# The second weight matrix scaled and centred along its rows, ahead of its transpose, in a two-layer hypergraph block

## The chip, the cores and the metric

The kernel runs on one core of a Trainium2 chip. Its five engines each work through their own instructions in order and meet only at semaphores: TensorE (PE in the profile), VectorE (DVE), ScalarE (ACT), GpSimd (POOL) and SyncE (SP, which here only issues transfers). The metric is the device time of one execution in microseconds (us), as the median of three runs.

## What is computed

The reference, cut to what matters. There are 64 graphs of 128 nodes, with 256 features in and out and 512 hidden ones. All is float32.

```python
def hypergraph_conv(x, adj, W, b):
    H = (adj != 0).astype(x.dtype)
    w = adj.reshape(N, -1)[:, :C]             # the first row of adj
    xw = jnp.einsum('ncd,hd->nch', x, W)
    Dn = 1 / einsum('nce,ne->nc', H, w)       # 0 where the sum is not positive
    Be = 1 / H.sum(axis=1)                    # 0 where the sum is 0
    m = Be[:, :, None] * jnp.einsum('nce,nch->neh', H, xw)
    return Dn[:, :, None] * jnp.einsum('nce,neh->nch', H, m) + b

h = relu(hypergraph_conv(x, adj, W1, b1))
h = (h - mean(h)) * rsqrt(var(h) + EPS_LN) * gamma + beta
y = hypergraph_conv(h, adj, W2, b2) + x
out = _layernorm(x + y)
```

The part that the change touches works on the weights alone. Since the normalised h is multiplied by W2, gamma can be folded into W2 (W2 times gamma, column by column), the subtraction of the mean of h can be folded in too (each output row of the scaled W2 less its own mean over the 512 hidden units), and beta gives one constant vector of 256 values, c2 = W2 beta, that is added to every row.

## The kernel before

The 64 graphs go in 16 groups of 4 (G, PER). For each group the kernel makes H, its transpose ht_sb, the matrix A = D H B H^T (make_s, then make_a, then transposed into at_sb), u = x^T A (make_u), v = W1 u (make_v, four chunks k of 128 hidden units, each six passes in a split of every operand into a high and a low half), r = relu(v) (ACT, L564), its split into r_hi (POOL, L1025) and r_lo (DVE, L751), g = r W2 (make_g, one call for each of the 4 graphs, 12 passes each, eight with r_hi and four with r_lo), the statistics of r from squares (sq_sb, pair_sb, q_sb, turn_q), y = A g (make_y), and the normalised output. Every engine's program is one list written out by hand; nothing reorders it. Groups are staggered: make_v of the next group is put between the make_g of this one.

Ahead of the loop stands a ramp, which fills this pipeline and prepares the weights. W1 is transposed (turn_w1) and split. W2 arrives as w2_raw with its 256 output rows in two blocks c of 128 partitions. In the kernel before, PE transposes it (turn_w2, L360) into PSUM; DVE multiplies by gamma on the way to w2_g (scale_w2, L806), since after the transpose the hidden unit is the partition and gamma a column of vec; the mean over the hidden units is then a sum over partitions, for which DVE adds the four chunks into one (w2_sum, L888 and L891), PE multiplies by a matrix of ones (sum_w2, L397) and DVE subtracts (centre_w2, L813); ACT rounds to w2_hi (L636) and DVE takes the rest, w2_lo (L819, w2_ready). c2 is made by PE from w2_t, the unscaled transpose that ACT copies out of PSUM (L631), and from beta_b, beta spread along the free axis by POOL (L1057): four matrix products (make_c2, L404), read by DVE (L824). b1, gamma and beta come by three small transfers, one transpose and one copy (vec).

In the PE program the ramp ends with make_v(0, 2), sum_w2, make_v(0, 3), make_c2 for two chunks, make_s(1), make_c2 for two chunks; then it waits for w2_ready, and the first make_g follows. Within the first pass of the loop (i = 0) stand turn_a(1), turn_h(2) and make_u(1) between the make_g, then turn_q(0), make_v(1, 0) and make_s(2).

Two waits stand at the join of ramp and loop. make_g of graph 0 waits chunk by chunk for r_hi and, in its last four passes, for r_lo of chunks 0 to 3. And relu(0, 3) on ACT must be done before POOL can make the fourth r_hi, after which DVE makes the fourth r_lo.

Of the kernel before, what the change touches and what calls it, by code (L numbers as in the profile page):

```python
# [5 lines left out]
ALU = mybir.AluOpType  # L6
# [5 lines left out]
P = 128  # L12
# [8 lines left out]
def hypergraph_block(nc, x, adj, W1, b1, gamma, beta, W2, b2, out):  # L21
# [13 lines left out]
    with ExitStack() as ctx:  # L35
# [15 lines left out]
        vec_rows = sb("vec_rows", [3 * KH, P])  # L51
        vec = sb("vec", [P, 3 * KH])
        w1_hi = sb("w1_hi", [P, KD, HID], F32R)
        w1_lo = sb("w1_lo", [P, KD, HID], F32R)
        w2_t = sb("w2_t", [P, KH, DOUT])
        w2_g = sb("w2_g", [P, KH, DOUT])
        w2_sum = sb("w2_sum", [P, KH // 2, DOUT])
        beta_b = sb("beta_b", [P, KH, P])
# [58 lines left out]
        turned_q = bank_g[:, PER - 1]  # L117

# [54 lines left out]
        def _(sp):  # L173
# [43 lines left out]
            load_x(1)  # L217
            sp.dma_start(b2_half[:, :], b2.unsqueeze(0).to_broadcast([P, DOUT])).then_inc(weights_in[3], 16)
# [30 lines left out]
        def _(pe):  # L249
# [41 lines left out]
            def make_v(i, k):  # L291
                if i == 0 and k < 2:
                    pe.wait_ge(w1_ready, k + 1)
                    pe.wait_ge(u_hi_ready, 1)
                elif k < 2:
# [87 lines left out]
            def make_first_u():  # L383
                pe.wait_ge(first_at, 1)
                pe.wait_ge(x_in[0], 16)
                for c in range(KD):
                    pe.wait_ge(vec_ready if c else edges_ready, 1)
                    for n in range(PER):
                        if n == PER // 2:
                            pe.wait_ge(at_ready, 1)  # L390
                        mm = pe.matmul(bank_g[:, c, graph(n)], x_sb[:, 0, n, graph(c)], at_sb[:, 0, n],  # L391
                                       start=True, stop=True)
                    mm.then_inc(u_made, 1)

            def sum_w2():
                pe.wait_ge(w2_added, 2)
                pe.matmul(bank_g[:, 0, 0:DOUT], ones[:, :], w2_sum[:, 0], start=True,  # L397
                          stop=True).then_inc(w2_summed, 1)
# [714 lines left out]
```

## Time and profile before

| | us |
|---|---|
| median of 3 runs | 284.51 (284.22 to 284.69) |
| the profiled execution, its own time | 284.18 |
| its span, first to last instruction | 282.4 |
| PE busy | 274.3 |
| DVE busy | 228.8 |
| ACT busy | 197.5 |
| POOL busy | 135.0 |

The span is the stretch in which the profile shows instructions; the execution's own time is 1.8 us longer. Busy time is the union of an engine's instructions. A timeline row gives the start, the duration, the engine, the line and the operation, the destination tile and the sources, and in brackets how long the engine had been idle before and what ended that. Names in it drop a tile's numbers: w_hi is w1_hi or w2_hi, c is c2, w_bn is w2_bn. A row that says x2 merges neighbours, and each float32 product shows as more than one pass. An instruction's recorded duration contains its latency, so the next one on the same engine can start some 0.05 to 0.1 us before its end.

### The profile page before, as it was taken

How to read it: one execution, taken by the hardware profiler on the slowest of the kernel's cores; microseconds unless marked ns; L12 is line 12 of the kernel's file. 1: busy time of each engine (PE TensorE's matmuls, PEld its weight loads, DVE VectorE, ACT ScalarE, POOL GpSimd, SP SyncE). 2: the span in 40 equal slices, each digit the busy share in tenths (PEclk: the TensorE clock that was granted, in tenths of full speed). 3: DMA queues.
4: the chain of work that ended last, by engine and by line, in shares of the span. 5: the costliest groups of instructions: out<-in, count | busy, mean ns of one | idle time of the engine just before them, and what ended most of it. 6: DMA issues, size and time to landing. Idle time of an engine off the chain costs nothing.

```text
span 282.4 us, 5790 instructions
## 1 busy us (share of the span) xinstructions
PE 274.3 (97%) x1820; PEld 249.1 (88%) x1820; DVE 228.8 (81%) x646; ACT 197.5 (70%) x561; POOL 135.0 (48%) x196
## 2 busy tenths in 40 slices
PE   7999999999999999999999999999999999999991
PEld 6889899898999989898998989899898989889891
DVE  3795689797878979797987979797897969797784
ACT  3588967877777787776767877677778776564733
POOL 2332546436363744536274553536364363627372
PEclk9999999999999999999999999999999999999997
DMA  6922041334324334433433533523323242120024
GB/s 216 329 56 76 3 130 37 95 113 131 115 59 138 84 93 120 127 114 84 144 62 99 134 100 112 124 85 56 126 63 93 79 111 77 37 74 3 1 75 149
DMA packets 37302, 27.70 MB, mean 98 GB/s; under 512 B 10060, under 2 KB 35352, under 8 KB 37272
## 3 DMA queue, kind: packets, MB, share of 16 engines
q1 hardware_dynamic: 37024, 27.17, 33.9%
q8 instruction: 14, 0.23, 0.4%
q10 hardware_dynamic: 248, 0.17, 0.2%
q14 instruction: 16, 0.13, 0.2%
HBM read 17.21 MB, written 8.42 MB: 91 GB/s over the span
## 4 chain that ended last, share of the span: by engine, by line
PE 86%; DVE 5%; ACT 4%; POOL 2%; issue 2%; POOLq 0%; DVEq 0%; ACTq 0%
PE bank_v L309 29%; PE bank_g L326 10%; PE bank_g L319 9%; PE bank_g L321 9%; PE bank_v L287 9%; PE bank_v L345 9%; PE bank_s L267 4%; PE bank_g L338 2%; PE bank_s L410 1%; DVE r_lo L751 1%; ACT ht_sb L513 1%; ACT sq_sb L571 1%; DVE pair_sb L756 1%; ACT r_sb L564 1%; PE bank_g L391 1%
## 5 line engine op out<-in xcount | busy, mean ns | idle before, releaser
L1017 POOL TENSOR_TENSOR xb_sb<-x_sb,b_half 128x512 f32<-128x512 f32 (+1 forms) x31 | 41.1, 1327 | 70.7 <-DVE r_lo L751 53.7
L564 ACT ACTIVATE r_sb<-bank_v,vec 128x512 f32<-128x512 f32 x64 | 44.2, 691 | 38.5 <-PE bank_v L309 37.9
L319 PE MATMUL bank_g<-w_hi,r_hi 128*128 128x258 f32 x256 | 66.8, 293 | 0.0
L1025 POOL TENSOR_SCALAR r_hi<-r_sb 128x512 fp32r<-128x512 f32 x64 | 43.8, 684 | 42.6 <-ACT r_sb L564 42.1
L321 PE MATMUL bank_g<-w_lo,r_hi 128*128 128x256 f32 x256 | 63.7, 281 | 0.0
L309 PE MATMUL bank_v<-u_lo,w_hi 128*128 128x512 f32 x128 | 50.8, 397 | 0.0
L309 PE MATMUL bank_v<-u_hi,w_lo 128*128 128x512 f32 x128 | 50.8, 397 | 0.0
L309 PE MATMUL bank_v<-u_hi,w_hi 128*128 128x512 f32 x128 | 50.7, 396 | 0.0
L319 PEld LDWEIGHTS bank_g<-w_hi,r_hi 128*128 128x128 f32 x256 | 48.3, 189 | 1.7 <-DVE w_lo L819 0.3
L321 PEld LDWEIGHTS bank_g<-w_lo,r_hi 128*128 128x128 f32 x256 | 48.2, 188 | 1.2
L751 DVE TENSOR_TENSOR r_lo<-r_sb,r_hi 128x512 fp32r<-128x512 f32 x64 | 48.7, 782 | 0.5 <-POOL r_hi L1025 0.5
L326 PE MATMUL bank_g<-w_hi,r_lo 128*128 128x258 f32 x256 | 42.1, 285 | 0.1
L571 ACT ACTIVATE sq_sb<-r_sb 128x512 f32<-128x512 f32 x64 | 40.2, 635 | 1.9
L742 DVE SCALAR_TENSOR_TENSOR g_sb<-bank_g,rstd,c 128x256 f32<-128x256 f32 x62 | 27.2, 480 | 12.2 <-POOL rstd L1001 12.2
L326 PEld LDWEIGHTS bank_g<-w_hi,r_lo 128*128 128x128 f32 x256 | 35.8, 189 | 0.5 <-DVE r_lo L751 0.5
L576 ACT ACTIVATE z_sb<-z_sb,shift,rstd 128x256 f32<-128x256 f32 x60 | 32.3, 587 | 2.7 <-POOL shift L1039 2.7
L542 ACT ACTIVATE u_hi<-bank_v 128x512 fp32r<-128x512 f32 x30 | 17.9, 601 | 21.6 <-PE bank_v L287 21.6
L1001 POOL TENSOR_TENSOR rstd<-stat,half_power 128x2 f32<-128x2 f32 x31 | 21.9, 708 | 17.3 <-DVE stat L732 17.2
L287 PE MATMUL bank_v<-at_sb,x_sb 128*128 128x128 f32 x240 | 29.5, 276 | 0.0
L309 PEld LDWEIGHTS bank_v<-u_lo,w_hi 128*128 128x128 f32 x128 | 24.0, 188 | 6.1 <-DVE u_lo L719 0.7
L345 PE MATMUL bank_v<-g_sb,at_sb 128*128 128x256 f32 x120 | 28.8, 380 | 0.0
L287 PEld LDWEIGHTS bank_v<-at_sb,x_sb 128*128 128x128 f32 x240 | 28.0, 192 | 0.5 <-issue 0.5
(124 smaller groups left out, 453.6 us busy)
## 6 DMA issues: line engine op xcount, KB each, us to landing
x_sb<-in_x_dram SPq DMA_DIRECT2D x16, 512.0 KB, 3.9
out_dram<-z_sb SPq DMA_DIRECT2D x14, 512.0 KB, 3.3
adj_sb<-in_adj_dram SPq DMA_DIRECT2D x15, 256.0 KB, 4.2
d_row<-d_rows SPq DMA_DIRECT2D x13, 256.0 KB, 3.7
w_raw<-in_L_gnn_W_dram SPq DMA_DIRECT2D x2, 512.0 KB, 4.9
out_dram<-z_sb SPq DMA_DIRECT2D x3, 256.0 KB, 2.1
adj_sb<-in_adj_dram SPq DMA_DIRECT2D x2, 128.0 KB, 2.3
turned_h<-h_sb SPq DMA_TRANSPOSE x13, 2.4
```

Of the source, the lines that this page charges most:

```text
L287: mm = pe.matmul(bank_v[:, c, graph(n)], x_sb[:, j % 3, n, graph(c)], at_sb[:, j % 3, n], start=True, stop=True)
L309: mm = pe.matmul(bank_v[:, k % 2], w[:, c, graph(k)], u[:, c], start=(m == 0), stop=(m == len(terms) - 1))
L319: pe.matmul(bank_g[:, n, 0:W2COLS], r_hi[:, i % 2, k, graph(n)], w2_hi[:, k], start=(k == 0), stop=False)
L321: pe.matmul(bank_g[:, n, 0:DOUT], r_hi[:, i % 2, k, graph(n)], w2_lo[:, k], start=False, stop=False, skip_group_check=True)
L326: mm = pe.matmul(bank_g[:, n, 0:W2COLS], r_lo[:, i % 2, k, graph(n)], w2_hi[:, k], start=False, stop=(k == KH - 1))
L345: mm = pe.matmul(bank_v[:, half, (n % 2) * DOUT:(n % 2 + 1) * DOUT], at_sb[:, i % 3, n], g_sb[:, n], start=True, stop=True)
L564: nc.scalar.activation(r_sb[:, k], bank_v[:, k % 2], ACT.Relu, bias=vec[:, k:k + 1]).then_inc(relu_ready, 1)
L571: nc.scalar.activation(sq_sb[:, k], r_sb[:, k], ACT.Square).then_inc(sq_ready, 1)
L576: ins = nc.scalar.activation(z_sb[:, i % 2, n], z_sb[:, i % 2, n], ACT.Identity, bias=shift2[:, n:n + 1], scale=rstd2[:, 0, n:n + 1])
L751: nc.vector.tensor_tensor(r_lo[:, i % 2, k], r_sb[:, k], r_hi[:, i % 2, k].bitcast(F32), ALU.subtract).then_inc(r_lo_ready, 1)
L1017: nc.gpsimd.tensor_tensor(xb_sb[:, i % 2, part], x_sb[:, i % 3, part], b2_half[:, :].unsqueeze(1).to_broadcast([P, n, DOUT]), ALU.add).the ...
L1025: nc.gpsimd.tensor_scalar(r_hi[:, i % 2, k], r_sb[:, k], 1.0, 1.0, ALU.mult, ALU.mult).then_inc(r_hi_ready, 1)
```

## The change

- **Loads.** gamma and beta are each loaded onto all 128 partitions (gamma_b, beta_b, 128x512) by SP, and only b1 comes by the small transfer. W2 comes in two transfers, one for each block of output rows. The order on SP is now: the two halves of adj 0, W1, gamma_b, x 0, adj 1, W2 block 0, W2 block 1, adj 2, x 1, beta_b, b2, and on as before.
- **W2.** POOL multiplies w2_raw by gamma_b (two TENSOR_TENSOR of 128x512). DVE takes each row's mean (mean_w2: one bn_stats over 512 and one bn_aggr for each block). POOL subtracts it (two TENSOR_SCALAR). PE transposes the finished matrix once (turn_w2), ACT rounds it out of PSUM to w2_hi, DVE takes w2_lo out of PSUM.
- **c2.** POOL multiplies w2_raw by beta_b. DVE takes row means (bn_stats, bn_aggr) and writes for each block a diagonal matrix with 512 times the mean (c2_diag). PE multiplies ones by the two diagonals (make_c2), which puts c2 on all partitions.
- **Orders.** make_first_u does both chunks of the first two graphs, then both of the last two. make_first_v replaces make_v(0, 0) and make_v(0, 1) and interleaves them. turn_h(1) stands ahead of them. turn_w2 moves behind make_v(0, 2), make_s(1) ahead of make_v(0, 3), turn_h(2) and turn_a(1) ahead of the first make_g, make_u(1) ahead of the second. make_c2 stands behind turn_q(0). The lists of ACT, DVE and POOL follow.

The core of the diff (the new tiles, semaphores and make_first_u are left out):

```diff
-            sp.dma_start(w2_raw[:, :, :], W2.rearrange("(k p) h -> p k h", p=P)).then_inc(weights_in[2], 16)
+            sp.dma_start(gamma_b[:, :], gamma.unsqueeze(0).to_broadcast([P, HID])).then_inc(gamma_in, 16)
             load_x(0)
             load_adj(1)
+            for c in range(KD):
+                sp.dma_start(w2_raw[:, c], W2[c * P:(c + 1) * P, :]).then_inc(w2_high_in if c else weights_in[2], 16)
...
-            def turn_w2(half):
-                pe.wait_ge(weights_in[2], 16)
+            def turn_w2(c):
+                pe.wait_ge(w2_centred, c + 1)
                 pe.wait_ge(ht_ready, 1)
...
+                for k in range(KH):
+                    mm = pe.transpose(w2_turned_in[:, k, graph(c)], w2_g[:, c, graph(k)], ident[:, :])
...
+            def make_c2():
+                pe.wait_ge(diag_ready, KD)
+                pe.wait_ge(at_ready, 2)
                 for c in range(KD):
...
+                    mm = pe.matmul(bank_q[:, graph(c)], ones[:, :], c2_diag[:, c], start=True, stop=True)
+                mm.then_inc(c2_made, 1)
...
             turn_first_a(0)
+            turn_first_a(1)
+            make_first_u()
+            turn_h(1)
+            make_first_v()
+            make_v(0, 2)
             turn_w2(0)
-            turn_first_a(1)
             turn_w2(1)
-            make_first_u()
-            make_v(0, 0)
-            turn_h(1)
-            make_v(0, 1)
-            make_v(0, 2)
-            sum_w2()
+            make_s(1)
             make_v(0, 3)
-            make_c2([0, 1])
-            make_s(1)
-            make_c2([2, 3])
+            turn_h(2)
+            turn_a(1)
...
             relu(0, 0)
-            read_ht(1)
             relu(0, 1)
...
+            make_htb(1)
             relu(0, 2)
-            make_htb(1)
-            act.wait_ge(w2_centred, 1)
-            nc.scalar.activation(w2_hi[:, :, 0:DOUT], w2_g[:, :, :], ACT.Copy).then_inc(w2_hi_ready, 1)
+            act.wait_ge(w2_turned, KD)
+            nc.scalar.activation(w2_hi[:, :, 0:DOUT], w2_turned_in, ACT.Copy).then_inc(w2_hi_ready, 1)
+            make_a(1)
             relu(0, 3)
-            make_a(1)
             read_at(1)
...
+            def sum_beta(c):
+
+                dve.wait_ge(beta_scaled, c + 1)
+                nc.vector.bn_stats(w2_bn[:, 1, c], w2_beta[:, c]).then_inc(c2_step, 1)
...
+            pool.wait_ge(gamma_in, 16)
+            for c in range(KD):
+                pool.wait_ge(w2_high_in if c else weights_in[2], 16)
+                nc.gpsimd.tensor_tensor(w2_g[:, c], w2_raw[:, c], gamma_b[:, :], ALU.mult).then_inc(w2_scaled, 1)
+            for c in range(KD):
+                pool.wait_ge(w2_mean_ready, c + 1)
+                nc.gpsimd.tensor_scalar(w2_g[:, c], w2_g[:, c], w2_mv[:, 0, c, 0:1], 1.0, ALU.subtract,
+                                        ALU.mult).then_inc(w2_centred, 1)
             for k in range(KH):
...
+                split_r(0, k)
+            pool.wait_ge(beta_in, 16)
+            for c in range(KD):
+                nc.gpsimd.tensor_tensor(w2_beta[:, c], w2_raw[:, c], beta_b[:, :], ALU.mult).then_inc(beta_scaled, 1)
```

PE before, from the last pass of make_v(0, 3) to the first make_g (w_t is w2_t, L404 is make_c2, L267 make_s(1)):

```order
L309 MATMUL bank_v<-u_lo,w_hi 128x512
L404 MATMUL bank_g<-w_t,beta_b 128x256 [waits w2_t_ready,beta_ready]
L404 MATMUL bank_g<-w_t,beta_b 128x256
L267 MATMUL bank_s<-htb_sb,ht_sb 128x129 [waits a_ready,at_ready,wcol_ready,htb_ready]
L267 MATMUL bank_s<-htb_sb,ht_sb 128x129 x3
L404 MATMUL bank_g<-w_t,beta_b 128x256 [waits w2_t_ready,beta_ready]
L404 MATMUL bank_g<-w_t,beta_b 128x256
L319 MATMUL bank_g<-w_hi,r_hi 128x258 [waits r_hi_ready,w2_ready]
```

PE now, from the last pass of make_v(0, 2) to the first of make_v(0, 3): the products for c2 are gone from here, W2's one transpose and make_s(1) stand ahead of make_v(0, 3).

```order
L311 MATMUL bank_v<-u_lo,w_hi 128x512
L361 MATMUL bank_g<-ident,w_g 128x128 [waits ht_ready,w2_centred]
L361 MATMUL bank_g<-ident,w_g 128x128 x3
L361 MATMUL bank_g<-ident,w_g 128x128 [waits ht_ready,w2_centred]
L361 MATMUL bank_g<-ident,w_g 128x128 x3
L276 MATMUL bank_s<-htb_sb,ht_sb 128x129 [waits a_ready,at_ready,wcol_ready,htb_ready]
L276 MATMUL bank_s<-htb_sb,ht_sb 128x129 x3
L311 MATMUL bank_v<-u_hi,w_hi 128x512 [waits relu_ready]
```

The products for c2, four of 128x256, are two of 128x128 now and stand behind turn_q(0).

POOL before, from beta_b to the first xb_sb:

```order
L1057 TENSOR_SCALAR beta_b<-ones,vec 128x128 [waits vec_ready,consts_ready]
L1057 TENSOR_SCALAR beta_b<-ones,vec 128x128 x3
L1061 TENSOR_SCALAR b_half<-b_half 128x256 [waits weights_in3]
L1063 TENSOR_SCALAR ident<-ident 128x128
L1025 TENSOR_SCALAR r_hi<-r_sb 128x512 [waits relu_ready,consts_ready]
L1025 TENSOR_SCALAR r_hi<-r_sb 128x512 [waits relu_ready] x3
L995 COPY htb_sb<-edge_cols 128x4 [waits s_made,edges_ready] x2
L1017 TENSOR_TENSOR xb_sb<-x_sb,b_half 128x512 [waits q_ready,x_in0]
L1017 TENSOR_TENSOR xb_sb<-x_sb,b_half 128x512 [waits b_ready]
```

POOL now, from the scaling of W2 to the first two xb_sb (w_g is w2_g, w_beta is w2_beta):

```order
L1064 TENSOR_TENSOR w_g<-w_raw,gamma_b 128x512 [waits weights_in2,gamma_in]
L1064 TENSOR_TENSOR w_g<-w_raw,gamma_b 128x512 [waits w2_high_in]
L1067 TENSOR_SCALAR w_g<-w_g,w_mv 128x512 [waits w2_mean_ready] x2
L1032 TENSOR_SCALAR r_hi<-r_sb 128x512 [waits relu_ready] x4
L1073 TENSOR_TENSOR w_beta<-w_raw,beta_b 128x512 [waits beta_in]
L1073 TENSOR_TENSOR w_beta<-w_raw,beta_b 128x512
L1075 TENSOR_SCALAR b_half<-b_half 128x256 [waits weights_in3]
L1077 TENSOR_SCALAR ident<-ident 128x128
L1002 COPY htb_sb<-edge_cols 128x4 [waits s_made,edges_ready,consts_ready]
L1002 COPY htb_sb<-edge_cols 128x4 [waits s_made,edges_ready]
```

The two products with gamma and the two subtractions stand ahead of the four r_hi of group 0, and the two products with beta right behind them.

DVE before, from the third and fourth r_lo of group 0 to the sum of squares:

```order
L751 TENSOR_TENSOR r_lo<-r_sb,r_hi 128x512 [waits r_hi_ready] x2
L824 COPY c<-bank_g 128x256 [waits c2_made]
L692 TENSOR_SCALAR h_sb<-adj_sb 128x512 [waits h_turned,adj_in0]
L711 TENSOR_SCALAR binv<-members 128x4 [waits ht_ready]
L714 RECIPROCAL binv<-binv 128x4 [waits htb_ready,b_step]
L756 TENSOR_TENSOR pair_sb<-sq_sb 128x512 [waits sq_ready] x2
L763 TENSOR_TENSOR q_sb<-pair_sb 128x512 [waits pairs_ready]
```

DVE now, from the fourth r_lo to the same place:

```order
L760 TENSOR_TENSOR r_lo<-r_sb,r_hi 128x512 [waits r_hi_ready]
L825 BN_STATS w_bn<-w_beta 128x6 [waits beta_scaled]
L827 BN_AGGR w_mv<-w_bn 128x2 [waits c2_step]
L829 TENSOR_SCALAR c_diag<-ident,w_mv 128x128 [waits c2_mean_ready]
L825 BN_STATS w_bn<-w_beta 128x6 [waits beta_scaled]
L827 BN_AGGR w_mv<-w_bn 128x2 [waits c2_step]
L829 TENSOR_SCALAR c_diag<-ident,w_mv 128x128 [waits c2_mean_ready]
L720 TENSOR_SCALAR binv<-members 128x4 [waits ht_ready]
L723 RECIPROCAL binv<-binv 128x4 [waits htb_ready,b_step]
L765 TENSOR_TENSOR pair_sb<-sq_sb 128x512 [waits sq_ready] x2
```

Six instructions for c2 stand between the fourth r_lo and the binv of group 2, ahead of the pairs of squares.

## Rows read from the trace of the kernel before

**Rows 1.** The profile page, first part: busy time, share of the span, instructions.

```profile
PE 274.3 (97%) x1820; PEld 249.1 (88%) x1820; DVE 228.8 (81%) x646; ACT 197.5 (70%) x561; POOL 135.0 (48%) x196
```

**Rows 2.** Busy time by stretch: window, length, then each engine's busy time and instructions.

```profile
60.00:100.00 40.00, 39.97 (x269) 36.72 (x268) 33.86 (x102) 29.16 (x88) 21.50 (x29) 1.00 0.35 98
```

**Rows 3.** Timeline of PE in the ramp: start us, us, line, operation, out<-in, count.

```profile
9.74 1.95 PE L391 MATMUL bank_g<-at_sb,x_sb 128*128 128x128 f32 x16
...
16.54 0.59 PE L397 MATMUL bank_g<-w_sum,ones 128*128 128x256 f32 x2
...
18.36 1.02 PE L404 MATMUL bank_g<-w_t,beta_b 128*128 128x256 f32 x4
19.22 1.06 PE L267 MATMUL bank_s<-htb_sb,ht_sb 128*128 128x129 f32 x8
20.11 1.03 PE L404 MATMUL bank_g<-w_t,beta_b 128*128 128x256 f32 x4
21.06 0.39 PE L319 MATMUL bank_g<-w_hi,r_hi 128*128 128x258 f32 x1
...
22.96 0.60 PE L275 MATMUL bank_s<-ident,a_sb 128*128 128x128 f32 x4
...
23.60 0.36 PE L319 MATMUL bank_g<-w_hi,r_hi 128*128 128x258 f32 x1
...
25.11 1.95 PE L287 MATMUL bank_v<-at_sb,x_sb 128*128 128x128 f32 x16
26.82 0.37 PE L319 MATMUL bank_g<-w_hi,r_hi 128*128 128x258 f32 x1
...
28.81 0.66 PE L338 MATMUL bank_g<-ident,q_sb 128*128 128x128 f32 x4 [0.32 <-DVE q_sb L763]
29.41 0.50 PE L309 MATMUL bank_v<-u_hi,w_hi 128*128 128x512 f32 x1
...
30.91 1.05 PE L267 MATMUL bank_s<-htb_sb,ht_sb 128*128 128x129 f32 x8
```

**Rows 4.** The chain that ended last, one piece: start us, us, what.

```profile
33.41 4.19 PE bank_v L309 x18
```

**Rows 5.** Timeline of ACT in the ramp, columns as in the third group.

```profile
10.84 0.60 ACT L542 ACTIVATE u_hi<-bank_g 128x512 fp32r<-128x512 f32 x1 [0.38 <-PE bank_g L391]
...
13.70 0.69 ACT L564 ACTIVATE r_sb<-bank_v,vec 128x512 f32<-128x512 f32 x1 [1.38 <-PE bank_v L309]
...
18.69 1.06 ACT L636 ACTIVATE w_hi<-w_g 128x1024 fp32r<-128x1024 f32 x1
...
21.52 1.14 ACT L530 ACTIVATE a_sb<-bank_s,dinv 128x128 f32<-128x128 f32 x4 [1.20 <-DVE dinv L706]
```

**Rows 6.** Timeline of DVE in the ramp and after it.

```profile
10.04 0.43 DVE L692 TENSOR_SCALAR h_sb<-adj_sb 128x512 bf16<-128x512 f32 x1 [0.47 <-DMA adj_sb<-in_adj_dram]
...
16.23 1.10 DVE L751 TENSOR_TENSOR r_lo<-r_sb,r_hi 128x512 fp32r<-128x512 f32 x1
...
21.40 1.28 DVE L751 TENSOR_TENSOR r_lo<-r_sb,r_hi 128x512 fp32r<-128x512 f32 x2
...
38.65 1.10 DVE L756 TENSOR_TENSOR pair_sb<-sq_sb 128x512 f32<-128x512 f32 x1
...
45.36 1.38 DVE L785 BATCH_NORM_STATS2 bn_sb<-z_sb 128x6 f32<-128x256 f32 x4
```

**Rows 7.** Timeline of POOL at the same places.

```profile
16.10 0.69 POOL L1025 TENSOR_SCALAR r_hi<-r_sb 128x512 fp32r<-128x512 f32 x1 [0.94 <-ACT r_sb L564]
...
21.43 1.30 POOL L995 COPY htb_sb<-edge_cols 128x4 f32<-128x4 f32 x2
...
38.40 0.81 POOL L1025 TENSOR_SCALAR r_hi<-r_sb 128x512 fp32r<-128x512 f32 x1 [0.65 <-ACT r_sb L564]
39.16 0.64 POOL L995 COPY htb_sb<-edge_cols 128x4 f32<-128x4 f32 x1
```

**Rows 8.** Groups of POOL's instructions with their shapes: count, busy us, mean ns.

```profile
L1017 POOL TENSOR_TENSOR xb_sb<-x_sb,b_half 128x512 f32<-128x512 f32 x30 | 38.7, 1292 | 68.0 <-DVE r_lo L751 53.7 <-DVE binv L714 8.1 <-DVE q_sb L763 6.2
```

More of the change, by code:

```diff
@@ L50, in hypergraph_block @@
         w2_raw = sb("w2_raw", [P, KD, HID])
-        vec_rows = sb("vec_rows", [3 * KH, P])
-        vec = sb("vec", [P, 3 * KH])
+        vec_rows = sb("vec_rows", [KH, P])
+        vec = sb("vec", [P, KH])
         w1_hi = sb("w1_hi", [P, KD, HID], F32R)
         w1_lo = sb("w1_lo", [P, KD, HID], F32R)
[L55 to L58, printed above, removed]
+        gamma_b = sb("gamma_b", [P, HID])
+        beta_b = sb("beta_b", [P, HID])
+        w2_g = sb("w2_g", [P, KD, HID])
+        w2_beta = sb("w2_beta", [P, KD, HID])
+        w2_bn = sb("w2_bn", [P, 2, KD, 6])
+        w2_mv = sb("w2_mv", [P, 2, KD, 2])
+        c2_diag = sb("c2_diag", [P, KD, P])
         w2_hi = sb("w2_hi", [P, KH, W2COLS], F32R)
@@ L291, in make_v @@
             def make_v(i, k):
[L292 to L295, printed above, removed]
+                if k < 2:
                     pe.wait_ge(u_lo_ready, i * KD + (k + 1))
@@ L385, in make_first_u @@
                 pe.wait_ge(x_in[0], 16)
-                for c in range(KD):
[L387 to L398, printed above, removed]
@@ L400, in make_c2 @@
-            def make_c2(chunks):
-                pe.wait_ge(beta_ready, 1)
-                pe.wait_ge(w2_t_ready, 1)
-                for k in chunks:
-                    mm = pe.matmul(bank_g[:, 1, 0:DOUT], beta_b[:, k], w2_t[:, k], start=(k == 0), stop=(k == KH - 1))
-                if chunks[-1] == KH - 1:
-                    mm.then_inc(c2_made, 1)
+                for half in range(2):
+                    for c in range(KD):
+                        if half:
+                            pe.wait_ge(at_ready, 1)
+                        else:
+                            pe.wait_ge(vec_ready if c else edges_ready, 1)
+                        for n in each(half):
+                            mm = pe.matmul(bank_g[:, c, graph(n)], x_sb[:, 0, n, graph(c)], at_sb[:, 0, n],
+                                           start=True, stop=True)
+                        if half:
+                            mm.then_inc(u_made, 1)
@@ new lines, in make_first_v, with add @@
+            def make_first_v():
+                def add(k, c, w, u, first=False, last=False):
+                    return pe.matmul(bank_v[:, k], w[:, c, graph(k)], u[:, c], start=first, stop=last,
+                                     skip_group_check=True)
+                pe.wait_ge(u_hi_ready, 1)
+                for k in range(2):
+                    pe.wait_ge(w1_ready, k + 1)
+                    add(k, 0, w1_hi, u_hi, first=True)
+                    add(k, 0, w1_lo, u_hi)
+                pe.wait_ge(u_lo_ready, 1)
+                for k in range(2):
+                    add(k, 0, w1_hi, u_lo)
+                pe.wait_ge(u_hi_ready, KD)
+                for k in range(2):
+                    add(k, 1, w1_hi, u_hi)
+                    add(k, 1, w1_lo, u_hi)
+                    pe.wait_ge(u_lo_ready, KD)
+                    add(k, 1, w1_hi, u_lo, last=True).then_inc(v_made, 1)
@@ L443, in _ @@
                 if i == 0:
-                    turn_a(1)
-                    turn_h(2)
-                    pe.wait_ge(c2_ready, 1)
+                    make_u(1)
                 make_g(i, 1)
-                if i == 0:
-                    make_u(1)
                 if i == LAST:
@@ L605, in _ @@
             act.dma_start(edge_rows[:, :], adj[:, 0, :]).then_inc(edges_in, 16)
[L606 to L608 removed]
+            act.dma_start(vec_rows[:, :], b1.rearrange("(k p) -> k p", p=P)).then_inc(weights_in[0], 16)
             act.wait_ge(consts_ready, 2)
@@ L1064, in _ @@
             pool.wait_ge(consts_ready, 5)
-            for k in range(KH):
-                split_r(0, k)
             copy_w(2)
```

92 lines of the change are left out of this document (37 added, 55 removed).

## The prediction, made before the changed kernel ran

> **What bounds the kernel now.** I read the share of busy time first: PE is busy for 274.3 of 282.4 us [rows 1]. Then the stretches: in the loop it is busy 39.97 of 40 us [rows 2], so there PE's own list is the time, and the change leaves the loop behind its first pass alone. What it can move is the ramp. So I read PE's timeline there and set a checkpoint that both kernels pass with the same PE work done and the same work left: the start of make_s(2), at 30.91 us [rows 3]. Whatever the changed kernel is earlier or later there, I carry unchanged to the end; a full PE list neither gives it back nor adds to it.
>
> **What the change takes from PE.** sum_w2 starts at 16.54 and make_v(0, 3) follows at 16.78, about 0.24 us; the next pass runs only after a wait for a relu, so another 0.2 there. The products for c2 hold 18.36 to 19.22 and 20.11 to 21.06, 0.86 + 0.95 = 1.81 us [rows 3]. The two new products of 128x128 are four passes like those of turn_a, which takes 22.96 to 23.40, 0.44 us [rows 3]. So PE has 0.24 + 1.81 - 0.44 = 1.6 us less to do. The eight transposes of W2 only move. The rest of the working is on how much of the 1.6 comes back as waiting.
>
> **The start.** SP now issues gamma_b (256 KB) where it issued W2 (512 KB), so x 0 and adj 1 come no later; adj 1 was used on landing at 10.04 [rows 6]. W2's blocks follow behind it, 256 KB each; from 10.0 on I give each about 0.9 us. On POOL a two-input product of 128x512 takes 1.29 us [rows 8]: blocks scaled by 11.5 and 12.8 or, with 0.5 us of lateness, 13.3. DVE comes to the first mean only behind u_lo, at about 13.0, so loads and scaling are covered by up to 1.4 us and cost nothing. On PE turn_w2 is gone ahead of make_first_u, which starts at 9.5 instead of 9.74 [rows 3], but its first chunk is complete only after 12 of 16 passes, not 8: u_hi starts at 11.05 instead of 10.84 [rows 5]. The twelve passes of make_first_v run from 11.8 at 0.233 us each (18 in 4.19 us, [rows 4]), without the old waits in between. relu(0, 0) starts at 14.25 where it started at 13.70, takes 0.69 [rows 5], and make_v(0, 2) waits for it: 15.1 to 16.5.
>
> **The middle, a chain through four engines.** DVE's mean: a bn_stats of 128x256 is a quarter of 1.38 us [rows 6], so 0.67 for 512 elements, and 0.2 for the small bn_aggr. The two means are done at 13.8 and 14.9, POOL's subtractions at 14.5 and 15.6 to 15.8 (0.62 us each, as an r_hi [rows 7]). PE wants the second at 16.9, so this is covered too. Then turn_w2 16.5 to 17.4, make_s(1) 0.89 us to 18.25, make_v(0, 3) to 19.65. The sums of make_s(1) are out at 18.5, three small DVE operations end at 19.1, make_a(1) takes 1.14 us [rows 5]. Because it now stands ahead of relu(0, 3) on ACT, that relu runs 20.1 to 20.8, although its input was ready at 19.95. turn_h(2) waits for the same make_a(1), 0.7 us of idle PE; turn_a(1) is done at 21.1. w2_hi and w2_lo come at 18.6 and 20.2 (their operations took 1.06 and 1.23 us) and are ahead of that. POOL makes the fourth r_hi by 21.5; make_h(3) is on DVE at the time, which may hold it up to 21.75.
>
> **The step that decides.** Right behind the fourth r_hi POOL starts the product with beta_b; DVE is to make the fourth r_lo, from two inputs in SBUF. In the trace POOL and DVE don't run such pairs side by side. The r_lo at 16.23 takes 1.10 us instead of 0.68, beside an r_hi from 16.10 to 16.79 [rows 6, 7]: it ends 0.54 after the other. The pair_sb at 38.65 does the same after the r_hi that ends at 39.21. Whoever comes second waits for the first's end. POOL starts its next instruction just ahead of its last one's end (0.05 us: 38.40 + 0.81 against 39.16 [rows 7]) while DVE must be told first. So POOL gets in, with an operation of 1.29 us: 21.7 to 23.0, and the fourth r_lo ends at 23.3 to 23.55. The trace has no such DVE instruction beside a POOL TENSOR_TENSOR of this size. The bounds for this wait are 0 (it runs undisturbed, ending at 22.5) and both POOL products, 2.55 us. I take one product, 1.25, since the pair_sb at 38.65 got its turn at the end of one instruction, ahead of the copy that POOL had begun at 39.16, which ended only at 39.80, after it [rows 6, 7].
>
> The Trainium skill, page "SBUF — State Buffer", section "Who interferes with whom", says that a DVE instruction with two SBUF inputs and a GpSimd instruction that reads SBUF exclude each other for the whole instruction, and that the one that issues first wins. The rows above agree at 0.62 us, and the page makes no exception for products; by it the wait is the 1.25 us that I take, without it the sum below would be 0.7 us better. It does not say who is next of two that wait.
>
> **From there to the checkpoint.** With the fourth r_lo at 23.5 the first make_g ends at 23.7. Before, it was followed by turn_a and turn_h and all were done at 23.60 [rows 3]: so the gain is used up, 0.1 us behind. make_u(1) takes 1.71 and a make_g 1.51 (25.11 to 26.82, 23.60 to 25.11): make_u and two make_g end at 23.7 + 4.73 = 28.45. Before, PE reached turn_q(0) only at 28.81, after 0.32 us of waiting for q_sb, and make_v(1, 0) at 29.41 behind u_lo [rows 3]. Now: c2's second product ends at 24.8 on POOL, DVE's six operations (2 x (0.67 + 0.2 + 0.25)) at 26.15, binv at 26.45, pairs and sum (3 x 0.6) at 28.3. So q_sb is just in time and turn_q(0) runs 28.45 to 28.9. The c2 products follow to 29.35, by when the first u_lo (28.9) is there. make_v(1, 0) takes 6 x 0.233 = 1.4 to 30.75, where it took 1.50. That is 0.16 us ahead of 30.91. Reading c2 on DVE ends at 29.9 and is covered by make_v(1, 0). At the profiled execution this gives 284.18 - 0.16 = 284.02; the median of the runs lies 0.33 above that execution, so I forecast 284.35.
>
> **The rivals.**
> - **No exclusion by a product.** The fourth r_lo ends at 22.5, one us earlier. Then the sum of squares becomes the bound: c2's DVE operations end at 25.45, q_sb at 27.65, turn_q(0) and c2 until 28.65, make_v(1, 0) until 30.05: 0.86 ahead, 283.65. Against it are rows of the same pair at a smaller size; for it, that the trace has no such case.
> - **POOL keeps its turn through both products (the other side).** In DVE's own case it is so: two r_lo run 21.40 to 22.68 back to back while POOL's copies wait from 21.43 to 22.73 [rows 6, 7]. If POOL does the same, the fourth r_lo ends at 24.8, the first make_g at 25.0, and the two make_g behind make_u(1) at 29.75, turn_q(0) and c2 at 30.65, make_v(1, 0) at 32.05: 1.14 behind, 285.65. It decides as soon as the second product starts ahead of the r_lo. Against it stands the copy at 39.16.
> - **The weights come late.** If the scaled block 0 isn't there at 13.0, every us beyond that moves the means, and beyond some 1.1 us for block 1 the transposes; the r_hi stand behind them on POOL. At 2 us of lateness this costs about 0.9, 285.4.
> - **The change doesn't do what it says**, in that PE's freed 1.6 us are waited away earlier and the exclusion adds to it, because the chain make_s(1), make_a(1), relu(0, 3) is longer than counted. Each 0.1 us there is 0.1 us at the end; this is the width of the main case, not a case of its own.
>
> **How the numbers follow.** Chances: the main case 0.60, no exclusion 0.22, POOL keeps its turn 0.13, late weights 0.05. In the main case some ten hand-overs are added up, the holding up by make_h(3) is 0 or 0.25, and adding a few tenths each way gives 283.8 to 284.9. The predicted time is the likeliest case's, 284.35. The range reaches into both others, 283.3 to 285.3: it leaves out most of the slower cases and the better half of an even larger gain, about 0.2. A measurement of this kernel tells 0.2%, 0.57 us, from no change. Faster by more than that: 0.12 of the main case and most of the second, 0.19, together 0.31. Slower by more: 0.05 of the main case and most of the last two, 0.15, together 0.20. Within it: 0.49.
>
> **What would show it.** The profile of the changed kernel should have the fourth r_lo of group 0 at 1.7 to 1.9 us instead of 0.68, beginning just behind POOL's first product with beta_b and ending about 0.54 after it. With 0.68 there the first rival holds, with 3 us the second. PE should stand idle some 0.7 us ahead of turn_h(2) and about one us within the first make_g, and make_s(2) should start at 30.7 or 30.8. turn_w2 without a wait shows that loads and means are covered. turn_q(0) should wait less than 0.2 us. A make_s(2) that is as forecast and a time that isn't would prove the carrying to the end wrong; a relu(0, 3) that begins before 19.9 or after 20.5 would prove the middle wrong.

## The result: 1.5 us slower, outside the range

The changed kernel takes 286.07 us (median of 4 runs, 285.95 to 286.24), the kernel before beside it 284.60 (4 runs, 284.22 to 284.71). The ratio is 1.0058, with a 95% interval of 1.0046 to 1.0070. (The ratios here and below are not the quotients of the two medians beside them and differ from those by up to 0.13%.) The forecast was 284.35 with a range of 283.3 to 285.3; the profiled execution of after took 285.95 us, with a span of 284.1. The busy shares, in the page's first part:

```profile
PE 272.1 (96%) x1814; PEld 247.8 (87%) x1814; DVE 230.0 (81%) x646; ACT 197.0 (69%) x560; POOL 142.0 (50%) x198
```

PE is busy 2.2 us less than in [rows 1], so what was to go (1.6 us by the forecast) is gone, and the span is 1.7 us longer. POOL is busy 7.0 us more, with 198 instructions instead of 196. The ramp on PE (start us, us, line, operation, tiles, count, and in brackets the idle time ahead and who ended it):

```profile
16.50 0.60 PE L361 MATMUL bank_g<-ident,w_g 128*128 128x128 f32 x4
18.06 0.66 PE L361 MATMUL bank_g<-ident,w_g 128*128 128x128 f32 x4 [0.96 <-POOL w_g L1067]
18.55 1.06 PE L276 MATMUL bank_s<-htb_sb,ht_sb 128*128 128x129 f32 x8
...
22.54 0.38 PE L266 MATMUL bank_s<-ident_b,h_sb 128*128 128x128 bf16 x4 [1.54 <-ACT a_sb L544]
...
25.62 0.39 PE L328 MATMUL bank_g<-w_hi,r_lo 128*128 128x258 f32 x1 [0.95 <-DVE r_lo L760]
25.84 1.95 PE L296 MATMUL bank_v<-at_sb,x_sb 128*128 128x128 f32 x16
...
30.52 0.60 PE L340 MATMUL bank_g<-ident,q_sb 128*128 128x128 f32 x4
30.95 0.61 PE L423 MATMUL bank_s<-c_diag,ones 128*128 128x128 f32 x4
...
32.79 1.05 PE L276 MATMUL bank_s<-htb_sb,ht_sb 128*128 128x129 f32 x8
```

The checkpoint, the last row, stands at 32.79 against 30.91 in [rows 3]: 1.88 us later. Between turn_w2 and the checkpoint PE waits three times: 0.96 between the two halves of turn_w2, 1.54 ahead of turn_h(2), 0.95 ahead of the last pass of the first make_g. POOL at the same place, which [rows 7] shows of before:

```profile
11.21 2.54 POOL L1064 TENSOR_TENSOR w_g<-w_raw,gamma_b 128x512 f32<-128x512 f32 x2 [5.54 <-DMA w_raw<-in_L_gnn_W_dram]
14.01 3.99 POOL L1067 TENSOR_SCALAR w_g<-w_g,w_mv 128x512 f32<-128x512 f32 x2 [0.26 <-DVE w_mv L815]
17.97 2.22 POOL L1032 TENSOR_SCALAR r_hi<-r_sb 128x512 fp32r<-128x512 f32 x3
23.05 0.71 POOL L1032 TENSOR_SCALAR r_hi<-r_sb 128x512 fp32r<-128x512 f32 x1 [2.86 <-ACT r_sb L578]
23.73 2.97 POOL L1073 TENSOR_TENSOR w_beta<-w_raw,beta_b 128x512 f32<-128x512 f32 x2
```

The second row is the surprise: two subtractions of the mean hold POOL for 3.99 us, 2.0 us each. The prediction had 0.62 each. The second ends at 18.00, and the three r_hi, two of which had their input from ACT by 15.6 and the third by 17.4, stand behind it. DVE (compare [rows 6]):

```profile
13.01 0.68 DVE L813 BATCH_NORM_STATS2 w_bn<-w_g 128x6 f32<-128x512 f32 x1
13.73 0.18 DVE L815 BATCH_NORM_AGGREGATE w_mv<-w_bn 128x2 f32<-128x6 f32 x1
...
14.89 0.41 DVE L701 TENSOR_SCALAR h_sb<-adj_sb 128x512 bf16<-128x512 f32 x1
18.63 2.11 DVE L760 TENSOR_TENSOR r_lo<-r_sb,r_hi 128x512 fp32r<-128x512 f32 x2 [3.33 <-POOL r_hi L1032]
...
21.05 0.16 DVE L715 SCALAR_TENSOR_TENSOR dinv<-bank_s,degree 128x4 f32<-128x4 f32 x1
...
23.79 1.77 DVE L760 TENSOR_TENSOR r_lo<-r_sb,r_hi 128x512 fp32r<-128x512 f32 x1 [0.51 <-POOL r_hi L1032]
```

DVE stands idle for 3.33 us until the first r_hi is there. Then two r_lo, held up by r_hi beside them, take 2.11 us and stand ahead of degree and dinv. So make_a(1) on ACT starts at 21.25 and relu(0, 3) behind it at 22.27 (compare [rows 5]):

```profile
14.26 1.32 ACT L578 ACTIVATE r_sb<-bank_v,vec 128x512 f32<-128x512 f32 x2 [0.97 <-PE bank_v L401]
...
21.25 1.14 ACT L544 ACTIVATE a_sb<-bank_s,dinv 128x128 f32<-128x128 f32 x4 [1.47 <-DVE dinv L715]
22.27 0.71 ACT L578 ACTIVATE r_sb<-bank_v,vec 128x512 f32<-128x512 f32 x1
```

Around and behind the checkpoint the delay stays what it is: turn_q of the 16 groups starts 1.71 us later than before for the first and 1.6 to 1.82 later for the others. The two profiled executions differ by 1.77 us (285.95 against 284.18), 0.11 less than the checkpoint; the two medians differ by 1.47, since the profiled execution of before is 0.42 below its median and that of the changed kernel only 0.12.

### The profile page after: what moved, and what is told of

It reads as the page before. It is cut to its first block, busy times and chain, and to the rows that moved or that the text cites. A ratio compares the mean times of both kernels' runs of the same rounds, so it can differ in the third digit from the quotient of the medians.

```text
span 284.1 us, 5774 instructions
## 1 busy us (share of the span) xinstructions
PE 272.1 (96%) x1814; PEld 247.8 (87%) x1814; DVE 230.0 (81%) x646; ACT 197.0 (69%) x560; POOL 142.0 (50%) x198
## 4 chain that ended last, share of the span: by engine, by line
PE 84%; DVE 5%; POOL 4%; issue 2%; DMA 2%; ACT 1%; SPq 1%; POOLq 0%; DVEq 0%
PE bank_v L311 28%; PE bank_g L328 10%; PE bank_g L321 10%; PE bank_g L323 10%; PE bank_v L296 9%; PE bank_v L347 9%; PE bank_s L276 4%; PE bank_g L340 2%; DMA x_sb<-in_x_dram 2%; POOL w_g L1067 1%; DVE r_lo L760 1%; POOL r_hi L1032 1%; POOL rstd L1039 1%; PE bank_g L393 1%; DVE bn_sb L976 1%
## 5 line engine op out<-in xcount | busy, mean ns | idle before, releaser
L760 DVE TENSOR_TENSOR r_lo<-r_sb,r_hi 128x512 fp32r<-128x512 f32 x64 | 50.4, 808 | 4.3 <-POOL r_hi L1032 4.3
L311 PE MATMUL bank_v<-u_hi,w_hi 128*128 128x512 f32 x124 | 49.3, 398 | 0.1
L311 PE MATMUL bank_v<-u_lo,w_hi 128*128 128x512 f32 x124 | 49.1, 396 | 0.0
L311 PE MATMUL bank_v<-u_hi,w_lo 128*128 128x512 f32 x124 | 49.0, 395 | 0.0
L311 PEld LDWEIGHTS bank_v<-u_lo,w_hi 128*128 128x128 f32 x124 | 23.3, 188 | 5.3
```

What stands on the lines that cost most here:

```text
L311: mm = pe.matmul(bank_v[:, k % 2], w[:, c, graph(k)], u[:, c], start=(m == 0), stop=(m == len(terms) - 1))
L760: nc.vector.tensor_tensor(r_lo[:, i % 2, k], r_sb[:, k], r_hi[:, i % 2, k].bitcast(F32), ALU.subtract).then_inc(r_lo_ready, 1)
```

## The experiments

**What POOL's subtraction costs.** The changed kernel with eleven operations put behind the last of POOL's program, each waiting for the one ahead of it, with DVE and ACT done; its total time says nothing.

```diff
+            form(dst, src, 1.0, 1.0, ALU.mult, ALU.mult)
+            form(dst, src, point, 1.0, ALU.mult, ALU.mult)
+            form(dst, src, point, 1.0, ALU.subtract, ALU.mult)
+            form(dst, src, 1.0, 1.0, ALU.subtract, ALU.mult)
+            form(dst, src, 1.0, 1.0, ALU.add, ALU.mult)
+            form(dst, src, point, 1.0, ALU.add, ALU.mult)
...
+            form(dst, src, point, None, ALU.subtract, None)
```

> The changed kernel with eleven more GpSimd TENSOR_SCALAR instructions behind its last one, one after another, on tiles that nothing uses any more; only their durations count, not the time. In the changed kernel the two subtractions (pointer scalar, subtract then mult, in place, 128x512) took 3.99 us together, an r_hi (immediates, mult then mult) 0.62. If the pointer scalar is the price: the mult with a pointer takes 1.3 to 2.0, a subtract or an add with an immediate 0.62. If the operation is the price: subtract with an immediate takes 2.0, mult with a pointer at most 1.3 (four of 128x128 took 1.60 in the kernel before). If working in place is the price: the same subtraction out of place takes 0.6 to 0.7.

Its timeline of POOL, each row one operation of 128x512, in the order of the diff (the scalar is the number 1.0 or, where mv_sb is among the inputs, one value for each partition):

```profile
281.73 0.62 POOL L1113 TENSOR_SCALAR sq_sb<-sq_sb 128x512 f32<-128x512 f32 x1 [0.75 <-DVE z_sb L994]
282.45 0.69 POOL L1113 TENSOR_SCALAR sq_sb<-sq_sb,mv_sb 128x512 f32<-128x512 f32 x1
283.24 2.00 POOL L1113 TENSOR_SCALAR sq_sb<-sq_sb,mv_sb 128x512 f32<-128x512 f32 x1
285.33 1.92 POOL L1113 TENSOR_SCALAR sq_sb<-sq_sb 128x512 f32<-128x512 f32 x1
287.34 0.62 POOL L1113 TENSOR_SCALAR sq_sb<-sq_sb 128x512 f32<-128x512 f32 x1
288.05 0.69 POOL L1113 TENSOR_SCALAR sq_sb<-sq_sb,mv_sb 128x512 f32<-128x512 f32 x1
...
292.94 1.57 POOL L1111 TENSOR_SCALAR sq_sb<-sq_sb,mv_sb 128x512 f32<-128x512 f32 x1
```

The value read from a partition costs 0.07 us, addition nothing, subtraction 1.3 us, whether it takes the number or the value. In place it takes 2.00 as well; at 128x128 it takes 0.72 where a product takes 0.37; as the instruction's only operation, with no product behind it, 1.57. So the price belongs to the operation subtract on this engine, not to the value per partition and not to working in place. Each form ran once; the two subtractions of the kernel itself, taken singly, show 2.01 and 2.00.

**The subtractions on DVE.** This and the next two kernels ran beside the kernel before at 284.24 us (19 runs).

```diff
                 nc.vector.bn_aggr(w2_mv[:, 0, c], w2_bn[:, 0, c]).then_inc(w2_mean_ready, 1)
+                dve.wait_ge(w2_mean_ready, c + 1)
+                nc.vector.tensor_scalar(w2_g[:, c], w2_g[:, c], w2_mv[:, 0, c, 0:1], None,
+                                        ALU.subtract).then_inc(w2_centred, 1)
...
-            for c in range(KD):
-                pool.wait_ge(w2_mean_ready, c + 1)
-                nc.gpsimd.tensor_scalar(w2_g[:, c], w2_g[:, c], w2_mv[:, 0, c, 0:1], 1.0, ALU.subtract,
-                                        ALU.mult).then_inc(w2_centred, 1)
```

> The changed kernel with the two subtractions of the mean on VectorE, right behind each mean, instead of on GpSimd. Theory that the mis-sized subtraction is the whole miss: the transpose of block 1 starts at 16.9 without a wait (18.06 in the changed kernel), the first r_hi at 15.0 (17.97), relu(0, 3) at 20.1 (22.27), make_s(2) at 30.8 (32.79), and the time is 286.07 - 2.0 = 284.1. Rival, that the exclusion beside the products with beta and the order of ACT hold the rest: only the 0.96 us of PE idle ahead of the transpose go, time 285.1.

284.45 us (10 runs, 284.00 to 284.82), ratio 0.9994 (0.9980 to 1.0009), against the 284.1 expected: the slowdown is gone, and so is any gain. DVE's row and PE's rows:

```profile
14.51 0.49 DVE L817 TENSOR_SCALAR w_g<-w_g,w_mv 128x512 f32<-128x512 f32 x1
...
22.17 1.77 DVE L760 TENSOR_TENSOR r_lo<-r_sb,r_hi 128x512 fp32r<-128x512 f32 x1 [0.51 <-POOL r_hi L1035]
```

```profile
10.13 2.02 PE L393 MATMUL bank_g<-at_sb,x_sb 128*128 128x128 f32 x16 [0.66 <-issue]
...
17.05 1.03 PE L361 MATMUL bank_g<-ident,w_g 128*128 128x128 f32 x8
```

The eight transposes stand in one row without a wait, and the fourth r_lo still takes 1.77. But make_first_u begins at 10.13, where the forecast had 9.5: x 0 was late. That is the next thing to explain (below).

**POOL's products with beta behind the fourth r_lo**, in the changed kernel and in the last one.

```diff
             pool.wait_ge(beta_in, 16)
+            pool.wait_ge(r_lo_ready, KH)
             for c in range(KD):
```

> The changed kernel with one more wait: GpSimd's products with beta start only when all four r_lo of group 0 are done. The fourth r_lo takes 0.68 instead of 1.77. Theory: the gain of 1.1 us there is lost at the sum of squares, since the products end 0.4 later and DVE's six operations for c2 stand ahead of it; PE waits about 1.1 us at turn_q(0), which starts at 30.5 to 30.7 (30.52), time 286.0. Rival, that the first make_g alone decides: make_s(2) 1.0 earlier, 285.1.

> Both edits together: the subtractions on VectorE, and the products with beta behind the four r_lo. Theory: as the first edit alone, 284.1, since the sum of squares is what comes last in both; turn_q(0) at 28.4 to 28.6. Rival, that the exclusion costs its 1.1 us at the end: 283.1.

They took 286.48 (4 runs, ratio 1.0075, 1.0060 to 1.0090) and 284.66 (10 runs, 1.0018, 1.0006 to 1.0031), where 286.0 and 284.1 were expected, and neither is better than its base. In the first:

```profile
24.14 0.69 DVE L760 TENSOR_TENSOR r_lo<-r_sb,r_hi 128x512 fp32r<-128x512 f32 x1 [0.51 <-POOL r_hi L1032]
```

```profile
31.03 0.66 PE L340 MATMUL bank_g<-ident,q_sb 128*128 128x128 f32 x4 [1.09 <-DVE q_sb L772]
```

With nothing of POOL beside it the r_lo takes 0.69, so the 1.77 was the product's doing. But the us is handed on, as expected: the products, the sums for c2 and q_sb come later, and PE waits 1.09 for q_sb, as it waits 1.08 in the second of the two. (The start of turn_q(0), 31.03, isn't to be held against the 30.52 of the changed kernel as it stands: this profiled execution begins make_first_u at 9.90, 0.34 later.)

**POOL adds the negated mean.** This and the next two ran beside the kernel before at 284.33 us (25 runs). DVE makes -mean (128x1, 0.15 us) and POOL keeps the work.

```diff
-                nc.gpsimd.tensor_scalar(w2_g[:, c], w2_g[:, c], w2_mv[:, 0, c, 0:1], 1.0, ALU.subtract,
+                nc.gpsimd.tensor_scalar(w2_g[:, c], w2_g[:, c], w2_neg[:, c:c + 1], 1.0, ALU.add,
```

> The changed kernel with the subtraction left on GpSimd, but done as the addition of the negated mean (one more small VectorE operation for each block). With the operation as the price, the two take 0.69 us each instead of 2.0, and the time is that of the kernel with the subtractions on VectorE, 284.3 to 284.7. With the pointer or the working in place as the price they stay at 2.0 and the time at 286.1.

284.55 us (10 runs, 284.22 to 285.00), ratio 1.0005 (0.9995 to 1.0014), as expected. An addition in place of the subtraction takes back the 1.5 us. This is the cleanest pair here, since both profiled executions begin make_first_u at nearly the same time (9.63 and 9.56) and POOL's list has the same order in both: the checkpoint stands at 31.14 against 32.79, 1.65 us earlier.

```profile
14.27 0.70 POOL L1071 TENSOR_SCALAR w_g<-w_g,w_neg 128x512 f32<-128x512 f32 x1 [0.47 <-DVE w_neg L818]
15.54 0.82 POOL L1071 TENSOR_SCALAR w_g<-w_g,w_neg 128x512 f32<-128x512 f32 x1 [0.56 <-DVE w_neg L818]
```

**gamma behind x 0 and adj 1**, with the subtractions on DVE. The issues of the first x_sb, with size and time to landing in us, in this order: the kernel before, the changed kernel, the one with the subtractions on DVE, and this one:

```profile
x_sb<-in_x_dram SPq DMA_DIRECT2D x1, 512.0 KB, 6.3
```

```profile
x_sb<-in_x_dram SPq DMA_DIRECT2D x1, 512.0 KB, 6.7
```

```profile
x_sb<-in_x_dram SPq DMA_DIRECT2D x1, 512.0 KB, 7.2
```

```profile
x_sb<-in_x_dram SPq DMA_DIRECT2D x1, 512.0 KB, 5.6
```

The same window of before and of the kernel with the subtractions on DVE (window, length, PE busy, granted clock, DMA share, GB/s):

```profile
6.00:8.00 2.00, 1.88 (x17) 1.00 1.01 339
```

```profile
6.00:8.00 2.00, 1.93 (x18) 1.00 0.90 224
```

gamma_b is among the loads under way in this window. It is half the size of W2's, which stood there before, but each of 128 partitions fetches the same row of HBM, and the core's whole traffic falls from 339 to 224 GB/s (247 in the changed kernel). With gamma's load later the slow window moves with it, from 6 to 8 (298 GB/s there) to 8 to 10:

```profile
8.00:10.00 2.00, 1.67 (x12) 1.00 0.92 246
```

The kernels with gamma ahead of x 0 have 322 to 363 GB/s from 8 to 10. And the landing isn't chance: in all six profiled executions with gamma ahead x 0 lands 6.7 to 7.2 us after its issue, in all three with gamma behind 5.4 to 5.6. Of before there is one profile, with 6.3 behind twice the bytes; against it this load holds up x 0 by 0.4 to 0.9 us.

```diff
-            sp.dma_start(gamma_b[:, :], gamma.unsqueeze(0).to_broadcast([P, HID])).then_inc(gamma_in, 16)
             load_x(0)
             load_adj(1)
+            sp.dma_start(gamma_b[:, :], gamma.unsqueeze(0).to_broadcast([P, HID])).then_inc(gamma_in, 16)
```

> The kernel with the subtractions on VectorE, and gamma's load onto all partitions issued behind x 0 and adj 1 instead of ahead of them. There x 0 landed 7.2 us after its issue, at 10.0, where it landed at 9.1 in the kernel before, and make_first_u started at 10.13. Theory that the broadcast holds the queue longer than its 256 KB tell: x 0 lands by 8.8, make_first_u starts at 9.5, bound by at_sb, and everything behind is 0.6 earlier: 283.9. Rival, that x 0's landing is chance from run to run: no difference, 284.45.

284.13 us (10 runs, 283.88 to 284.48), ratio 0.9995 (0.9986 to 1.0005). That is between the 283.9 of the theory and the 284.45 of its rival, and the time alone doesn't decide; the landing and the checkpoint, at 30.51 and 0.65 earlier than with gamma first, do. Of before the checkpoint is 0.40 ahead, which the runs can't tell from nothing.

```profile
30.51 1.05 PE L276 MATMUL bank_s<-htb_sb,ht_sb 128*128 128x129 f32 x8
```

**The products with beta in gaps of POOL.** To the last kernel: the first product ahead of the first r_hi, the second between the third and the fourth, and beta loaded ahead of x 1.

```diff
             pool.wait_ge(beta_in, 16)
             for k in range(KH):
+                if k in (0, KH - 1):
+                    c = k // (KH - 1)
+                    nc.gpsimd.tensor_tensor(w2_beta[:, c], w2_raw[:, c], beta_b[:, :],
+                                            ALU.mult).then_inc(beta_scaled, 1)
                 split_r(0, k)
```

> The kernel with gamma's load later, and the two products with beta moved into gaps of GpSimd: the first ahead of the first r_hi, the second between the third and the fourth r_hi; beta's load is issued one place earlier. Theory: the fourth r_lo takes 0.68 instead of 1.77 and the operations for c2 are no later than before, so PE neither waits 0.95 in the first make_g nor at turn_q(0), and make_s(2) is 1.0 to 1.1 earlier than in the kernel with gamma's load later: 282.9 if that one is at 283.9. Rival, that the products in the gaps hold up the first r_hi or the third r_lo by as much: no difference.

283.80 us (10 runs, 283.05 to 284.25), ratio 0.9976 (0.9965 to 0.9987): faster than the kernel before, by a quarter of a per cent, the best of all here, but 0.9 us above the 282.9 expected. make_s(2) starts at 30.33, only 0.18 earlier than in the kernel with gamma's load later, where 1.0 to 1.1 was expected: what the fourth r_lo no longer loses is lost elsewhere, as the rival had it. Its timelines of DVE and PE:

```profile
14.45 1.25 DVE L720 TENSOR_SCALAR binv<-members 128x4 f32<-128x4 f32 x1
...
22.23 0.88 DVE L760 TENSOR_TENSOR r_lo<-r_sb,r_hi 128x512 fp32r<-128x512 f32 x1 [0.51 <-POOL r_hi L1035]
```

```profile
17.28 0.66 PE L361 MATMUL bank_g<-ident,w_g 128*128 128x128 f32 x4 [0.30 <-DVE w_g L817]
```

The fourth r_lo takes 0.88, and the last pass of the first make_g doesn't wait. But binv, an operation on four numbers a partition, takes 1.25 us instead of 0.16 because it met the first product (14.20 to 15.66), and the second mean stands behind it.

**The first product moved behind the second r_hi**, to spare binv (beside the kernel before at 284.60, 17 runs).

```diff
-                if k in (0, KH - 1):
-                    c = k // (KH - 1)
+                if k in (KH - 2, KH - 1):
+                    c = k - (KH - 2)
```

> The kernel before this one (beta_in_gaps, 283.8) with POOL's first product with beta moved from ahead of the first r_hi to behind the second, where POOL stood idle 0.97 us in the kernel with gamma issued later; the second product stays ahead of the fourth r_hi. Nothing else is changed. My theory: what that kernel lost was binv (L720), which took 1.25 us instead of 0.16 because it met the first product, and with it the second mean, the transposes and make_a(1), 0.5 to 0.7 us in all; the fourth r_lo was no longer held up. So here binv is 0.16 us again, the eight transposes stand without a wait, the fourth r_lo takes 0.69 to 0.9 us and ends at 22.3 to 22.6 instead of 23.1, make_s(2) starts 0.5 to 0.9 us earlier than 30.33: median 283.1 to 283.3. Rival: a product anywhere in the ramp meets some operation of DVE, here the first r_lo and the operations on degree behind it (18.4), which then end 0.5 us later and pass it on to make_a(1) in the same way: 283.7 to 284.0, no difference.

284.20 us (12 runs, 283.88 to 286.44), ratio 0.9999 (0.9981 to 1.0016): no gain. Nine runs took 283.88 to 284.5, one 285.7 and two 286.4. The nine alone, sorted out after the fact, have a median of 283.93, near the 283.80 of the products in gaps, so that the rival of no difference holds for them too. The profiled execution is one of the two slowest, and it shows how this program loses some 2.5 us. POOL, DVE, PE, and the last row as a window of PE (length, PE busy, granted clock, DMA share, GB/s):

```profile
16.17 1.45 POOL L1072 TENSOR_TENSOR w_beta<-w_raw,beta_b 128x512 f32<-128x512 f32 x1
17.60 0.79 POOL L1035 TENSOR_SCALAR r_hi<-r_sb 128x512 fp32r<-128x512 f32 x1
18.36 1.71 POOL L1072 TENSOR_TENSOR w_beta<-w_raw,beta_b 128x512 f32<-128x512 f32 x1
```

```profile
16.41 1.50 DVE L701 TENSOR_SCALAR h_sb<-adj_sb 128x512 bf16<-128x512 f32 x1
17.83 1.09 DVE L760 TENSOR_TENSOR r_lo<-r_sb,r_hi 128x512 fp32r<-128x512 f32 x1
```

```profile
18.85 1.77 DVE L760 TENSOR_TENSOR r_lo<-r_sb,r_hi 128x512 fp32r<-128x512 f32 x1
```

```profile
22.42 0.38 PE L266 MATMUL bank_s<-ident_b,h_sb 128*128 128x128 bf16 x4 [2.70 <-ACT a_sb L544]
```

```profile
24.00:26.00 2.00, 2.00 (x12) 0.50 0.39 85
```

Three operations of DVE in a row meet three of POOL, each ends a little after the one of POOL it waited for (18.39 + 0.54 for the first r_lo, 20.07 + 0.54 for the second), and degree comes at 20.54. PE waits 2.70 us, and then, a second loss, its granted clock is 0.50, the lower level of 1.2 GHz, from 23 to 26. From turn_h(2) to make_s(2), with the same program, it takes 10.59 us (22.42 to 33.01) where it takes 9.35 with the products in gaps (20.98 to 30.33), at a clock of 1.00: so the clock costs about 1.2 us. In the changed kernel the longest wait of the ramp was 1.54 us and the granted clock stayed 1.00 behind it.

No fast run of this kernel was profiled, so what sends a run down this road is not shown. In this profile W2 is late: POOL begins to scale it at 11.98 (11.69 with the products in gaps) and the first mean waits 0.34 us for it, which puts h_sb just behind the start of the product. Nor is this kernel alone in having stragglers: two of the 19 runs of the kernel before in one group took 285.5 and 285.6, and one of 10 with the subtractions on DVE and the products behind the four r_lo took 286.2. These have no profile.

## Why the prediction was wrong

- **The step that failed: "POOL's subtractions at 14.5 and 15.6 to 15.8 (0.62 us each, as an r_hi)".** They take 2.0 each and end at 16.02 and 18.00, and by the forecast's own sign, a relu(0, 3) after 20.5, the middle was wrong. "PE wants the second at 16.9, so this is covered too" falls with it: turn_w2's second half waits 0.96, and make_s(1) starts at 18.55 instead of 17.4. The r_hi on POOL's queue behind the subtractions are the second way: the two held-up r_lo end at 20.7 where make_s(1)'s sums were there about a us earlier, and relu(0, 3) starts at 22.27 instead of 20.1, 2.2 late. The checkpoint is 2.04 late (32.79 against 30.75). The kernel in which only this term is mended, by addition, has it at 31.14. So 1.65 of the 2.04 are this term. (The kernel with the subtractions on DVE, at 31.16, agrees partly by luck: it started 0.57 later than the changed kernel and gained on the first r_lo, as the next two points tell.) I had taken an r_hi as the nearest row: same engine, form and size, another operation. The kernel before has no subtraction on POOL, and I put no bounds on the term.
- **A second size off: the start.** "x 0 and adj 1 come no later" was reckoned by bytes. x 0 lands 0.4 (here) to 0.9 us later after its issue than before. make_first_u started at 9.56 in the profiled execution, near the forecast 9.5, but at 10.13 with the subtractions on DVE and at 9.42 with gamma later. W2 was scaled later than I had it, too: the second block at 13.75 instead of 12.8 to 13.3. That cost nothing, since DVE came to it only at 14.09.
- **The rest of the middle: 0.4 us short.** With the term mended by addition, relu(0, 3) starts at 20.62, not 20.1: the first two r_lo take 2.11 for 1.27, since the r_hi come in a row behind the second addition. I had let neither hold the other up there. In the kernel with gamma's load later, where these two take 1.27 and the start is at 9.42, relu(0, 3) starts at 20.00.
- **The step that decides was right**, in size and in order: the fourth r_lo takes 1.77 (forecast 1.7 to 1.9), in four kernels, and ends 0.54 behind the end of POOL's first product; 0.69 where the product waits. DVE got its turn before the second product, so that "POOL keeps its turn" is out, and its 285.65 is nearest to the result by luck. What spoke for that rival was a misread row: the 1.30 us of POOL's copies from 21.43 in [rows 7] is two copies merged. Singly they are

```profile
21.43 0.70 POOL L995 COPY htb_sb<-edge_cols 128x4 f32<-128x4 f32 x1
22.07 0.66 POOL L995 COPY htb_sb<-edge_cols 128x4 f32<-128x4 f32 x1
```

  and each ends 0.05 us behind one of the two r_lo from 21.40 (the first ends at 22.08, the second at 22.68). So DVE didn't keep its turn there either, as far as these rows show: the engines took turns.
- **Also right:** relu(0, 0) at 14.26 (14.25), the means at 13.9 and 15.0 (13.8 and 14.9), turn_q without a wait, c2's products in 0.37 us, 0.07 less than turn_a's, and the carrying of the checkpoint to the end.
- **The forecast itself** is near what the kernel does once its subtraction costs what I had assumed: 284.45 and 284.55 against 284.35, no change within 0.2%. Part of that is luck: the checkpoint of those kernels is 0.4 us later than forecast, and the kernel before, on whose 284.51 the forecast was built, took 284.24 and 284.33 beside them. Why no gain comes of 1.6 us less work on PE: the ramp is bound by a chain through PE, DVE, ACT and POOL, and the time that PE no longer works there it spends waiting. Taking the exclusion away by a later product moved the wait to q_sb. The nearest to the first rival (the fourth r_lo undisturbed, 283.65) is the kernel with the products in gaps, at 283.80, and it needed the better order of loads as well.

## What to carry to other kernels

An operation that the trace doesn't show is priced with both its engine and its arithmetic: the row of another operation of the same form is no price, and the text must then carry an upper bound, here for a queue with four engines behind it. Where POOL only needs x - m, give it -m and let it add. In a ramp that is a chain, count what a removed piece of work leaves waiting before counting what it frees, and look at which operations of DVE stand beside each of POOL's: in one order of them here the time varied by 2.5 us from run to run, for a reason that stays open.

## What the runs showed of the hardware that I had not expected

- **Subtraction on POOL** at 128x512: 2.00 us (1.92 with a number, 1.57 alone) against 0.62 to 0.69 for product and sum; at 128x128 0.72 against 0.37. DVE does the same subtraction in 0.49. The Trainium skill, page "GPSIMD Engine Reference", section "4.1 Engine selection", has one-input elementwise work (it names add, multiply and maximum) on this engine as roughly line-rate. The rows at 0.62 against DVE's 0.49 agree with that. The subtraction, which it doesn't name, is far from it: four times DVE's time.
- **A subtraction on POOL didn't hold DVE up:** make_h (h_sb, L701) at 14.89, in the midst of POOL's subtractions from 14.01 to 18.00, takes 0.41, and so it does in the two other profiled executions with these subtractions. Beside an r_hi the same operation takes 0.85 (with the subtractions on DVE), beside a product with beta 1.50. No run here says why.
- **The exclusion takes turns** in every row above in which one of the two waits: it runs when the other's instruction ends, ahead of that engine's next, and an operation as small as binv (128x4) is held up until a product's end (1.25 us). The Trainium skill, page "SBUF — State Buffer", section "Who interferes with whom", says that tensor_scalar on DVE, in its two-port modes, is excluded as well, for the whole of a GpSimd instruction that issued first. The rows of binv and make_h beside a product agree, though the trace doesn't show the mode; make_h beside a subtraction doesn't, and there the measurement decides.
- **A load of one row to all partitions** takes more of the queue than its bytes tell: 224 and 247 GB/s in its window against 339, and 246 where the load was moved to.
- **PE's clock:** behind a wait of 2.70 us it was 0.50 for three us, behind one of 1.54 us 1.00.
